# Layer 2 outputs of a four-layer model: the router's weights of a token picked by one float32 product of 128 rows, and the order of three interleaved parts laid out anew

## The reference, cut to what matters

```python
# x: (4096 tokens, 128); HID = 176; NUM_EXPERTS, TOP_K = (8, 2)
scores = sigmoid(xf @ gate_w.T)
_, sel = top_k(scores + expert_bias, 2)
routed_in = xf[token] * scores[token, expert]          # float32 product, then bfloat16
h = square(relu(bf16(routed_in) @ bf16(w_up[expert])))  # as bf16
routed_out = h @ bf16(w_down[expert])                   # rounded to bf16
shared_out = square(relu(xf @ shared_w_up.T)) @ shared_w_down.T
out = sum over the two experts of routed_out + shared_out
x = x + s * silu(out)      # s: residual + y @ out_w, y from the readout
```

## Time and profile before

| | |
|---|---|
| median of 3 runs | 3510.58 us (3499.16 to 3518.64) |
| profiled execution | 3497.14 us, its span 3495.0 us |
| mean granted clock of PE | 0.822 |
| PE busy | 2496.2 us, 71% of the span |
| DVE busy | 2591.9 us, 74% |
| ACT busy | 1611.6 us, 46% |
| the stage `outputs2` after its loads | 2014.5 to 2325.7 us of the span |

### The profile page before, as it was taken

The page is one execution under the profiler, slowest core; times in us unless marked ns, Lnnn a source line. Parts: engine busy times, 40 slices in busy tenths (PEclk is TensorE's granted clock), DMA queues, the critical chain, the costliest instruction groups (busy, mean ns, idle before and its releaser), DMA issues.

```text
span 3495.0 us, 39641 instructions
## 1 busy us (share of the span) xinstructions
PE 2496.2 (71%) x13665; PEld 1325.7 (38%) x13665; DVE 2591.9 (74%) x5752; ACT 1611.6 (46%) x2999; POOL 513.6 (15%) x530
## 2 busy tenths in 40 slices
PE   3698877768687696886641078875787777778778
PEld 1343433333343333432220022212565555555554
DVE  3478869999999999998977657662666666666663
ACT  1333353443534425343332145553666666666662
POOL 0000003030030300303022000030212222121210
PEclk9678887889788788887865556556999999999999
DMA  3000010100101011010010121015777777776751
GB/s 87 2 9 29 19 41 7 51 15 28 37 7 47 13 32 33 5 47 22 29 28 13 27 63 52 9 38 148 221 209 207 206 212 209 207 218 202 207 151 50
DMA packets 311634, 282.67 MB, mean 81 GB/s; under 512 B 16296, under 2 KB 286266, under 8 KB 309994
## 3 DMA queue, kind: packets, MB, share of 16 engines
q1 hardware_dynamic: 311434, 280.15, 28.0%
HBM read 149.35 MB, written 122.36 MB: 78 GB/s over the span
## 4 chain that ended last, share of the span: by engine, by line
DVE 37%; PE 33%; issue 13%; ACT 10%; POOL 5%; DMA 2%; SPq 1%; DVEq 0%; POOLq 0%; ACTq 0%
PE banks L2613 4%; DVE t L2590 3%; PE banks L2657 3%; ACT t L2525 2%; PE banks L2230 2%; DVE t L999 1%; PE banks L2574 1%; DVE t L1668 1%; DVE t L1147 1%; DVE t L996 1%; POOL t L2557 1%; DVE t L1672 1%; PE banks L420 1%; DVE t L1662 1%; DVE t L1665 1%
## 5 line engine op out<-in xcount | busy, mean ns | idle before, releaser
L2613 PE MATMUL banks<-ident,t 128*128 128x128 f32 x2304 | 389.0, 289 | 136.0 <-ACT xT L2628 47.9
L2590 DVE CUSTOM_DVE_ANT_0 t<-banks,t 128x896 f32<-128x896 f32 (+7 forms) x512 | 381.6, 753 | 134.9 <-PE banks L2576 75.3
L2601 ACT ACTIVATE t<-t 128x896 f32<-128x896 f32 (+7 forms) x512 | 398.6, 779 | 175.4 <-DVE t L2590 174.7
L2613 PEld LDWEIGHTS banks<-ident,t 128*128 128x128 f32 x2304 | 258.0, 144 | 242.8 <-ACT xT L2628 63.7
L2557 POOL TENSOR_TENSOR t<-t 128x512 f32<-128x512 f32 x96 | 122.2, 1273 | 775.9 <-DMA t<-relative_scratch 651.5
L145 ACT ACT_TABLE_LOAD x127 | 162.9, 1283 | 151.3 <-DMA t<-in_fu 23.8
L2574 PE MATMUL banks<-t 128*128 128x512 bf16 (+3 forms) x768 | 214.5, 335 | 8.6 <-DVE t L2590 8.6
L1708 ACT ACTIVATE t<-t 128x16 f32<-128x16 f32 x256 | 82.5, 322 | 278.3 <-DVE t L1672 232.9
L1095 ACT ACTIVATE t<-banks 128x512 f32<-128x512 f32 x128 | 76.3, 596 | 222.5 <-PE banks L1061 222.0
L538 POOL TENSOR_TENSOR t<-t 128x512 f32<-128x512 f32 x28 | 50.2, 1791 | 873.6 <-ACT t L510 873.6
L1066 PE MATMUL banks<-t 128*128 128x512 f32 x256 | 145.9, 653 | 31.1 <-DVE t L1143 24.2
(11 more groups left out here) (454 smaller groups left out, 6181.2 us busy)
## 6 DMA issues: line engine op xcount, KB each, us to landing
relative_scratch<-t SPq DMA_DIRECT2D x128, 512.0 KB, 5.2
t<-relative_scratch SPq DMA_DIRECT2D x128, 512.0 KB, 4.4
relative_scratch<-t SPq DMA_DIRECT2D x128, 256.0 KB, 5.5
t<-in_wmoe SPq DMA_DIRECT2D x64, 384.0 KB, 3.1
t<-relative_scratch SPq DMA_DIRECT2D x80, 256.0 KB, 2.9
t<-cut_scratch SPq DMA_DIRECT2D x192, 64.0 KB
t<-t SPq DMA_DIRECT2D x16, 512.0 KB, 4.2
cut_scratch<-t SPq DMA_DIRECT2D x8, 768.0 KB, 3.5
```

The source lines that it names most:

```text
L2590: nc.vector.tensor_tensor_reduce(s.s[z][:, 0:n], ps[:, b0:b0 + 1 + i // 4, :].rearrange("p b n -> p (b n)")[:, 0:n], s.bias[r][:, j, WIDE ...
L2601: nc.scalar.activation(s.s[z][:, 0:n], s.s[z][:, 0:n], ACT.Exp, scale=-1.0, bias=s.least[:, z:z + 1]).then_inc(*a.mark("weights", u))
L2613: nc.tensor.transpose(ps[:, 4 + c % 2, (t - lo) * P:(t - lo + 1) * P], s.s[u % NS][:, t * P:(t + 1) * P], k.ident[:]).then_inc(*e.mark("tu ...
```

## The change

The three-part split goes. `comb` stays float32, is transposed as such on PE against the float32 identity, and is copied into the first 8 rows of a `combT` of 128 rows whose other 120 rows are zero. `pick` is float32 with 128 rows of which the first 8 are the identity. A pick is then one float32 product of 128 rows and 512 columns. Four DVE steps for each half and batch go; two memsets of `combT` and one of `pick` are new, and the bfloat16 identity is gone. The three strings of the order are new: the whole readout of the next batch (its products, squares, root and DVE steps) now stands in the prologue and just behind it, and the pairs of the loop follow each other in one pattern.

```diff
 def outputs2_loads_dve(k, s):
     nc, dve, v = k.nc, k.dve, k.line("out2_dve")
+    nc.vector.memset(s.pick[:], 0.0).then_inc(*v.mark())
+    for h in range(2):
+        nc.vector.memset(s.half[h].combT[:], 0.0).then_inc(*v.mark())
     dve.wait_ge(k.queue("o2_loads"), "all")
-    nc.vector.tensor_copy(s.pick[:], s.f_pick[:]).then_inc(*v.mark())
-    nc.vector.tensor_copy(s.ident_b[:], k.ident[:]).then_inc(*v.mark())
+    dve.wait_ge(v)
+    nc.vector.tensor_copy(s.pick[0:E2], s.f_pick[0:E2]).then_inc(*v.mark())
...
     def pick(x):
-        mm(bank(ps, bb), s.pick[:, x:x + 1].broadcast_to([3 * E2, P]), o.combT[:], start=True, stop=True).then_inc(
+        mm(bank(ps, bb), s.pick[:, x:x + 1].broadcast_to([P, P]), o.combT[:], start=True, stop=True).then_inc(
             *e.mark("pick", b, x))
...
     for t in range(NT):
-        mm(ps[0:3 * E2, bb, t * P:(t + 1) * P], o.parts[:, t].rearrange("p c e -> p (c e)"), s.ident_b[:], start=True, stop=True).then_inc(
-            *e.mark("comb", b))
+        nc.tensor.transpose(ps[0:E2, bb, t * P:(t + 1) * P], o.rb.comb[:, t], k.ident[:]).then_inc(*e.mark("comb", b))
...
-    nc.scalar.copy(o.combT[:], ps[0:3 * E2, bb, :]).then_inc(*a.mark("combT", b))
+    nc.scalar.copy(o.combT[0:E2], ps[0:E2, bb, :]).then_inc(*a.mark("combT", b))
...
-    nc.vector.scalar_tensor_tensor(o.rb.comb, o.rb.rank, 2.0, o.rb.score, ALU.is_lt, ALU.mult).then_inc(*v.mark())
-    yield
-    dve.wait_ge(v)
-    copy(o.parts[:, :, 0], o.rb.comb).then_inc(*v.mark())
-    yield
-    dve.wait_ge(v)
-    tt(o.rb.comb, o.rb.comb, o.parts[:, :, 0], ALU.subtract).then_inc(*v.mark())
-    yield
-    dve.wait_ge(v)
-    copy(o.parts[:, :, 1], o.rb.comb).then_inc(*v.mark())
-    yield
-    dve.wait_ge(v)
-    tt(o.parts[:, :, 2], o.rb.comb, o.parts[:, :, 1], ALU.subtract).then_inc(*v.mark("comb", b))
+    nc.vector.scalar_tensor_tensor(o.rb.comb, o.rb.rank, 2.0, o.rb.score, ALU.is_lt, ALU.mult).then_inc(*v.mark("comb", b))
...
-    s.wr, s.ebias, s.pick, s.ident_b = sb([P, E2]), sb([P, E2]), sb([3 * E2, E2], BF16), sb([P, P], BF16)
+    s.wr, s.ebias, s.pick = sb([P, E2]), sb([P, E2]), sb([P, E2])
...
-        o.rb, o.lg, o.parts, o.combT = route_buffers(sb, E2), sb([P, NT, E2]), sb([P, NT, 3, E2], BF16), sb([3 * E2, TB], BF16)
+        o.rb, o.lg, o.combT = route_buffers(sb, E2), sb([P, NT, E2]), sb([P, TB])
```

More of the change, by code:

```diff
@@ L2330 @@
 TURNS3_PE = (
-    "abrrrrrrrrraaabbbrraarbabbaaababbrbaaabbabbaaabbabbaaabbabbaababbabaaabbbarbaaarabbbbaaabbabbaabbabrraabbabaaaba"
-    "bbrbaaabbbabaaabbbrabbbaaabbraraaabbbabaaabbabbaaaaababbabbbababaabbbrraaarbbbabaabbabrabababbaaaabbbabaaabbabba"
-    "aabbbabaaabbabbbbaaabbaaabbababaaabbbaaabbaaabbabbbaaabbabbaaabbabbaaabbbabaaabbabbaaabbabbaaabbabbaabbabab"
+    "rabrrrrrrrraabbarrabrababarbbaaabbrbraaaabbbbaaababbbaaababbbaaababbbaaababbbaaababbbaabbababababarrbraababrabab"
+    "aabrbbraaababbbaaababbbaaababbbaaababbbaaabbabbaaabbabbaabbababababarrbraababrabbaaabbbaaaabbbbaaaabbbaabaabbbab"
+    "aaabbbaabaabbbaabaabbbabaabbababaabbbaaaabbbaababbabaaabbbabaaabbbabaaabbbabaaabbbaabaabbbabaaabbbabaabbabb"
 )
 TURNS3_ACT = (
-    "abrrrrrrrrrraarbrbrraabbrrrarabbaababbaababbaababbaabbabraabbabaaabbbaaabbabbabarbrabrraabbaabrbraabbarbraabbabr"
-    "bbaabaaabbabaababbaaaabababbbababbaabrrbrraabbrrrrabababbabaraabbabaabbabaabbabaababbbbaabaaababbababaabbaabbaab"
-    "baababbaabbabaabbabaababbaababbaababbaabbababab"
+    "rabrrrrrrrrrarrbarrabrarbrrbraabbaaabbbaababbaababbaababbaababbaababbaababbababrrabarrbrrararbbraabbaababbaababb"
+    "aababbaababbaababbaababbaababbababrrabarrbrrararbbraabbaaabbbaaabbabaabbabaabbabaabbabaabbabaabbababaabbbaabbaab"
+    "abaabbabaabbabaabbabaabbabaabbabaabbaababbabbab"
 )
 TURNS3_DVE = (
[L2343 to L2346, removed]
+    "rabrrrrrrrrrrrrraaaabababababbbrrbaarbabrrrrrbrarararbrbbaaaabbbbaaababbbaaababbbaaababbbaaababbbaaababbbaababba"
+    "bababababababrarabababbaarbrarrrrbrbrarararbbbaaababbbaaababbbaaababbbaaababbbaaababbbaaababbbaababbabababababab"
+    "abrarabababbaarbrarrrrbrbrarararbbbaaaabbbabaaabbbabaaabbbabaaabbbabaaabbbabaaabbbabaabbabaabaaaaababababbababbb"
+    "babbaababbabaaabbbabaaabbbabaaabbbabaaabbbabaaabbbabaaabbbaababbabbabab"
 )
```

## The result

The changed kernel took 3459.3 us (median of 4 runs, 3459.0 to 3460.8); the kernel before 3510.0 us (3499.2 to 3518.6). The ratio is 0.9856, 95% interval 0.9832 to 0.9881: faster by 1.4%. The profiled execution has a span of 3457.2 us against 3495.0, which is 37.8 us less.

A forecast was written before the change was run, and what follows sets the result against it. PE, busy but at half clock, was taken to bound the loop. Pairs -31.7, comb chain -3, readout +2 and prologues -6 gave about -38 us: 3472 us from the 3510.6 median (3459 from the profiled execution), range 3442 to 3520.

The forecast's parts named there:

- The clock: In the loops, full 128-row products kept streaming lift PE's clock from 1.2 GHz and it stays up.
- The clock rival: Loops stay at 1.2 GHz, a pair takes 8.1 us, total 3584 us, slower; chance 0.13 in all, 0.03 of it half-way.
- The pick: One float32 pick in the loop takes 1.0 us at 2.4 GHz, 1.9 at 1.2 GHz; 128 rows cost nothing.
- The pair: A pair of the loop goes from 6.09 to 5.1 us (4.56 to 5.6); over 32 pairs -31.7 us.
- PE's floor of 4.56: Rival: PE's need sets the loop's pair at 4.56 us and the readout hides; -60, 3450 us; chance 0.10.
- The readout's steps, moved: Next batch's readout leaves three loops for the place where the loop begins; together +2 us (-8 to +14).
- prologues: Prologues begin at the higher clock, against gaps at the loops' heads; together -6 us (-12 to +2).
- comb chain: Four DVE split steps leave the chain the prologue waits for, transposes replace four products; -3 us (-6 to 0).
- +12 and +4: Costs at the loops' heads: +12 us for moved readout steps queued on DVE, +4 for clock falls in PE's gaps.
- the -10 for the steps that leave the loops: Readout steps leaving the loops save about 3.4 us for each of three batches, -10.
- Hand-offs: Rival: the clock rises but DVE's strict order keeps a pair at 5.8 us; about 3503 us; chance 0.15.
- The signs: Loop clock 0.9 or more, durations 0.39, picks 1.0 us, six pairs about 31 us, stage 250, DVE busy 80%.

The follow-up runs named there:

- run 1: The changed kernel with its float32 picks cut from 128 to the 8 rows that hold something; 3565 us, ratio 1.016 to the kernel before.
- run 6: The kernel before with the new order, bfloat16 picks and second down products filled to 128 rows; 3447 us, ratio 0.9825.
- Run 3: The changed kernel's float32 picks of 128 rows, without the split, in the old order of the strings; 3467 us, ratio 0.9895.
- runs 9 to 12: The changed kernel again, 3460 us; it with down products filled to 128 rows, 3444 and again 3441; run 6 with shared way down filled too, 3455.
- run 4: The kernel before, order and bfloat16 split kept, with pick and combT zero-filled from 24 to 128 rows; 3460 us, ratio 0.9878.
- run 8: The changed kernel with the 64 float32 picks of layer 1's experts also filled from 8 to 128 rows; 3462 us, ratio 0.9870.

## Why the prediction was right, and where it was not

*The clock.* Right in its mechanism, and shown by runs: 8, 64 and 128 rows of the same product, 8 of them in use each time, give loops at 0.50 to 0.53, at 0.53 (once 0.93) and at 0.90 to 0.96. The doubt that rows of zeros might not count is settled. The clock rival did not happen, but at 64 rows three of four loops are what it describes. The rule of the Trainium skill that I set against the row (TensorE: Matmul & The Clock Gate, Part 1: sustained PE activity releases the throttle) does not hold here by busy time alone: 98% busy at 0.50 (run 1), 71% busy at 0.98 (run 6).

*The pick.* Forecast 1.0 us at 2.4 GHz; 0.86 where the next weights are ready. "That its rows are 128 and not 24 costs nothing" was too careful: full rows are cheaper. I had taken the bfloat16 products at 0.32 us as their price, and a third of it was weight loads that wait when the shape of the weights changes from one product to the next. With weights of 128 rows and 128 columns on both sides a product is followed after 0.22 to 0.23.

*The pair.* Forecast 5.1 (4.56 to 5.6), measured 4.39 where the clock is at 2.4 GHz, below the range, and 4.55 in the mean of all loops, at its lower end. The mis-sized term: 32 x (6.09 - 4.55) = -49 us in place of -31.7. Two causes: the durations above took 0.30 off PE's floor of 4.56 (4.26 busy in the four pairs shown), and the idle time of 0.54 on top of it, carried over from the old pair, shrank to 0.13. Run 3 points to the order for the second: in the old strings the same picks give a pair of 5.13 us, and the stage is 13 us longer. Filled down products took a further 0.3 off (runs 9 to 12), which is why "the shortest pair is 4.56" was no floor.

*The readout's steps, moved*, and the *prologues*. Forecast +2 and -6. With the comb chain's -3 that is -7; the stage gave 46.9 and the pairs 49 of it, so what is left for all else is +2. From first out product to first up product the prologues took 21.1, 20.0, 22.3 and 17.7 us, 81 against 84 before, some 3 less where -9 was forecast for prologues and comb chain; that the gain of the higher clock went in part into readout work ahead of the loop is likely, but not measured by itself. From first up to first down product it is 5.4, 7.8, 5.8 and 4.6 us, against 4.9, 5.3, 4.2 and 5.1 before: +5 in the three batches with a readout. In batch 2, PE's row, and DVE's two wide steps of the readout that the square stands between:

```profile
2196.08 1.14 PE L2232 MATMUL banks<-t 128*128 128x512 bf16 x2 [2.70 <-DVE t L2305]
```

```profile
2194.48 1.22 DVE L2154 TENSOR_TENSOR t<-t 128x1024 f32<-128x1024 f32 x1
2195.61 0.41 DVE L2305 TENSOR_TENSOR t<-t 48x512 bf16<-48x512 bf16 x1
2195.95 1.27 DVE L2158 SCALAR_TENSOR_TENSOR t<-t 128x1024 f32<-128x1024 f32 x1
```

```profile
2193.00:2203.00 10.00, 7.30 (x13) 1.99 (x13) 8.22 (x14) 3.46 (x6) 0.00 (x0) 0.66 0.00 0
```

The gap of 2.70 us goes with some us at the lower clock, and the loop with it is the one at 0.90. I had priced both (+12 and +4), and the cost in front of the loops came out smaller; of the gains set against it, the -9 of prologues and comb chain came out as some -3, and the -10 for the steps that leave the loops can't be told apart in the pairs.

*The comb chain.* Four transposes take 0.60 us at 2.4 GHz where four bfloat16 products took 0.39; that is inside the -3, which was not measured by itself.

*The sum.* -38 forecast for the profiled execution, -37.8 measured, and this agreement is partly luck: the stage gave 46.9, and 8.7 went to the later start, which the prediction did not speak of. Against the median it is -50.7, and the time of 3459 us lies 13 below the 3472 and inside the range. The kernel before had been profiled in one of its faster executions. By the prediction's own ends, first out product to PE's last, the stage went from 288.5 to 241.7 us, where about 250 was forecast; that difference of 8 is what the mis-sized pair gave beyond the terms that came out smaller.

*The rivals.* Hand-offs (5.8 us a pair) did not happen. PE's floor of 4.56, given 0.10, is what happened in the loops (4.55), and it deserved more: the pair of 4.17 us was better evidence than today's idle time. Its total of -60 did not follow, because the readout did not hide. The signs came as written (clock 0.90 to 0.96, durations 0.39 and 0.40, DVE busy 83% of the last loop), but for the six pairs, 26.5 us in place of 31, and the picks, 0.86 in place of 1.0.

## What to carry to other kernels

Read PE's granted clock next to its busy share. Where PE bounds a stretch, is busy and is still at half clock, look at the rows of its products. Filling the short ones with zeros to 128 costs a memset of each buffer, once; here it was worth 1.2% by itself (run 4) and, of all products of a pair and with the new order, 1.8% (run 6). In a part where DVE has the most to do it brought nothing (run 8). An order is worth another sum when the products around it change (-13 us with the new picks, +7 with the old), so it has to be tried again behind such a change.

## What the runs showed of the hardware that was not expected

Number of rows and clock, loops entered at 2.4 GHz: with 8 rows the clock is lost even where no readout follows (0.52); with 64 it is kept there (0.93), but once lost it stays at 0.50 for 57 us of nearly gapless work; with 128 it comes back within 7 us. This is read from one execution of each kernel.

A bfloat16 product of 512 columns is followed after 0.22 to 0.23 us at 2.4 GHz where its weights and the next ones are both 128*128, and after 0.31 to 0.33 where the shape changes, the load standing in between (PEld waits 0.23 us). It is not the rows alone: an up product of 128*48 weights is followed by one of 128*128 after 0.33 (2089.41 to 2089.74), both with 128 rows. Filling 48 rows to 128 took 0.3 us off a pair of 4.39.

Layers 0 and 1, untouched, are about 12 us longer in some executions than in others (the stage's first out product at 2046 to 2049 us against 2034 to 2037, once 2042), with a clock of 0.69 in place of 0.87 over the same 60 us. What tips it was not tried.
